# Attention in runs of two steps: a changed order of scores, row maxima and values on one core

## What is computed

```python
x = group_norm(input, gn_weight, gn_bias)            # B = 2, C = 128, 32 x 32
qkv = einsum('bchw,oc->bohw', x, qkv_weight)
q, k, v = split(qkv.reshape(B, 4, 96, 32, 32), 3, axis=2)
attn = einsum('bnchw,bncyx->bnhwyx', q, k) / sqrt(C)
attn = softmax(attn over all 1024 places y, x)
out = einsum('bnhwyx,bncyx->bnchw', attn, v).reshape(B, C, 32, 32)
out = einsum('bchw,oc->bohw', out, out_weight) + out_bias
x = out + input
# then: t = tokens(x); t = t + linear_attention(layer_norm(t)); t = t + experts(layer_norm(t))
```

## Time and profile before

| | |
|---|---|
| median of 3 runs | 360.91 us (359.94 to 361.03) |
| the profiled execution | 360.62 us, span 358.9 us |
| PE busy | 315.1 us (88%) |
| DVE busy | 202.1 us (56%) |
| ScalarE busy | 194.5 us (54%) |
| GpSimd busy | 113.7 us (32%) |
| steps 0 to 31, with row maxima | some 45 to 132 us of the span |
| steps 32 to 63, with layer 1 of image 0 | 132 to 203 us |

### The profile page before, as it was taken

One profiled execution on the slowest core, in us unless ns is written; L12 is line 12 of the kernel. 1 busy time (PEld: TensorE's weight loads), 2 busy tenths in 40 slices (PEclk: granted clock), 3 DMA queues, 4 the chain that ended last, 5 costly groups with the idle time before them and its releaser, 6 DMA issues.

```text
span 358.9 us, 6251 instructions
## 1 busy us (share of the span) xinstructions
PE 315.1 (88%) x1885; PEld 197.5 (55%) x1885; DVE 202.1 (56%) x620; ACT 194.5 (54%) x303; POOL 113.7 (32%) x190
## 2 busy tenths in 40 slices
PE   7979898899999989999999878796545599999986
PEld 3533443343444435355443336785444499999985
DVE  2585456475766753465747746766752057776610
ACT  1470676477676754546667320647332277777722
POOL 2073094000000000100031884015277745656630
PEclk9995999899999999999999998897858599999999
DMA  6069785835000007000000112100011422224215
GB/s 197 4 132 207 161 206 234 231 87 211 2 2 3 3 18 219 0 2 1 2 0 0 55 37 61 38 0 22 10 52 52 111 61 63 76 76 132 77 55 211
DMA packets 20540, 27.88 MB, mean 78 GB/s; under 512 B 3831, under 2 KB 14508, under 8 KB 20252
## 3 DMA queue, kind: packets, MB, share of 16 engines
q1 hardware_dynamic: 15800, 17.57, 18.3%
q0 software_dynamic: 3520, 9.39, 8.3%
q10 hardware_dynamic: 1188, 0.53, 0.6%
HBM read 11.15 MB, written 8.33 MB: 54 GB/s over the span
## 4 chain that ended last, share of the span: by engine, by line
PE 63%; issue 11%; POOL 11%; DVE 8%; ACT 3%; DMA 3%; SPq 0%; DVEq 0%; ACTq 0%; POOLq 0%
PE ps L913 14%; POOL expert_in L530 9%; PE ps L1132 8%; PE ps L1112 8%; PE ps L890 8%; PE ps L871 4%; PE ps L855 4%; PE ps L750 2%; PE ps L790 2%; PE ps L822 2%; POOL rstd L466 1%; DMA Qs<-mrow 1%; DVE pm L1247 1%; PE ps L1091 1%; PE ps L1163 1%
## 5 line engine op out<-in xcount | busy, mean ns | idle before, releaser
L598 ACT ACTIVATE probs<-ps 128x1024 f32<-128x1024 f32 x64 | 65.3, 1020 | 35.1 <-PE ps L890 35.0
L913 PE MATMUL ps<-probs,vT 128*32 128x512 f32 x256 | 68.6, 612 | 0.6 <-ACT probs L598 0.5
L913 PE MATMUL ps<-probs,ones 128*32 128x512 f32 x256 | 68.6, 612 | 0.0
L466 POOL TENSOR_TENSOR rstd<-ve,minus_half 128x1 f32<-128x1 f32 (+2 forms) x6 | 10.3, 1724 | 147.4 <-DVE ve L1298 77.3
L1112 PE MATMUL ps<-w,GT 128*128 x312 | 45.9, 294 | 12.0 <-ACT GT L728 11.7
L1244 DVE CUSTOM_DVE_ANT_0 above<-ps,above 128x512 f32<-128x512 f32 x56 | 38.6, 691 | 29.9 <-PE ps L871 27.4
L1112 PEld LDWEIGHTS ps<-w,GT 128*128 128x128 f32 x312 | 41.5, 207 | 13.6 <-issue 13.5
L1132 PE MATMUL ps<-XTT,w1s 128*128 128x128 f32 x312 | 46.2, 296 | 2.9 <-issue 2.7
L536 POOL DMA_INDIRECT token_out<-Y,yidx x39 | 37.7, 966 | 33.4 <-DVE Y L1571 28.7
L890 PE MATMUL ps<-Qs,Ks 98*128 98x512 f32 x128 | 43.6, 421 | 2.3 <-DMA Qs<-mrow 1.6
L1132 PEld LDWEIGHTS ps<-XTT,w1s 128*128 128x128 f32 x312 | 42.6, 211 | 4.3 <-issue 3.9
(11 more groups left out here) (224 smaller groups left out, 440.1 us busy)
## 6 DMA issues: line engine op xcount, KB each, us to landing
XR<-expert_in SPq DMA_DIRECT2D x39, 65.0 KB, 1.9
Qs<-q_hi SPq DMA_DIRECT2D x16, 128.0 KB, 3.1
w<-in_L_ffn_W SPq DMA_DIRECT2D x1, 2048.0 KB, 8.5
w<-in_L_ffn_W SPq DMA_DIRECT2D x8, 256.0 KB, 4.5
YG<-token_out SPq DMA_DIRECT2D x8, 256.0 KB, 3.9
Ks<-k_hi SPq DMA_DIRECT2D x14, 128.0 KB, 2.7
expert_in<-zeros POOLq DMA_DIRECT2D x1, 1300.0 KB, 5.6
expert_in<-zeros POOLq DMA_DIRECT2D x1, 1235.0 KB, 8.1
```

The source lines that it names most:

```text
L598: nc.scalar.activation(probs[:, s % 3, :], bank(2 + 2 * (s % 2), 2), ACT.Exp).then_inc(exp_done, 1)
L913: last = nc.tensor.matmul(bank(value_bank(o))[i * HD:(i + 1) * HD, :], w, probs[:, s % 3, hd * HALF:(hd + 1) * HALF], start=kt == 0, stop= ...
```

## The change

The order in which PE, ScalarE and DVE walk through the steps; no operation is added or removed. `pair_slots(s)` gives the new slots of steps s and s + 1 together, four or three.

- PE goes by two steps: first product of the first slot, scores of s + 1, its second product; first product of the second slot, scores of s + 2, its second product; then both products of the third and of the fourth slot; then, with the parts of layer 1 that belong to each, the values of s and the values of s + 1.
- ScalarE takes the positive parts of the first two slots behind the exp of the even step and those of the others behind the exp of the odd step; a part of layer 1 stands ahead of them.
- The "rows" of block 1 stand one place sooner in the list of slots.
- DVE's copy of the summed values stands behind the step's slots instead of behind its first one.

```diff
@@ order of slots
         for k in range(1, 2 * UNITS):
-            order.insert(min(RING * (k + 1) + 2, len(order)), (k, "rows"))
+            order.insert(min(RING * (k + 1) + (1 if k == 1 else 2), len(order)), (k, "rows"))
...
+        def pair_slots(s):
+            return range(slots_by(s), slots_by(s + 2))
@@ ScalarE
             for s in range(UNITS * STEPS):
                 exps(s // STEPS, s % STEPS)
-                if s:
-                    for g in new_slots(s - 1)[1:]:
-                        max_above(g)
                 run_parts(layer1, LAYER1_AT, s, 0)
-                for g in new_slots(s)[0:1]:
+                for g in pair_slots(s - 1)[2:] if s % 2 else pair_slots(s)[0:2]:
                     max_above(g)
@@ PE
-            for s in range(UNITS * STEPS):
-                new = new_slots(s)
-                for g in new[0:1]:
-                    max_first(g)
-                if s + 1 < UNITS * STEPS:
+            def both_scores(s):
+                if s < UNITS * STEPS:
                     for hd in range(2):
-                        scores((s + 1) // STEPS, (s + 1) % STEPS, hd)
-                for g in new[0:1]:
-                    max_second(g)
-                for g in new[1:2]:
-                    max_first(g)
-                if s == BEGIN_LAYER1:
-                    pe.wait_ge(consts_ready, 2)
-                    pe.wait_ge(ld_rows, 16 * 4)
-                run_parts(layer1, LAYER1_AT, s, 0)
+                        scores(s // STEPS, s % STEPS, hd)
+
+            def both_values(s):
                 for hd in range(2):
                     values(s // STEPS, s % STEPS, hd)
-                for g in new[1:2]:
-                    max_second(g)
+
+            for s in range(0, UNITS * STEPS, 2):
+                new = pair_slots(s)
+                for i in range(2):
+                    for g in new[i:i + 1]:
+                        max_first(g)
+                    both_scores(s + 1 + i)
+                    for g in new[i:i + 1]:
+                        max_second(g)
                 for g in new[2:]:
                     max_first(g)
                     max_second(g)
+                run_parts(layer1, LAYER1_AT, s, 0)
+                both_values(s)
+                if s + 1 == BEGIN_LAYER1:
+                    pe.wait_ge(consts_ready, 2)
+                    pe.wait_ge(ld_rows, 16 * 4)
+                run_parts(layer1, LAYER1_AT, s + 1, 0)
+                both_values(s + 1)
@@ DVE
                     norm_sums(o)
-                if s % KT == KT - 1 and s // KT < COPIED:
-                    values_copy(s // KT)
                 for g in new[1:2]:
                     max_slot(g)
...
                 for g in new[3:]:
                     max_slot(g)
+                if s % KT == KT - 1 and s // KT < COPIED:
+                    values_copy(s // KT)
```

## The result

The changed kernel took 367.37 us (median of four, 365.09 to 369.02) against 360.97 for the kernel before on the same chip, a ratio of 1.0196 (95% interval 1.0155 to 1.0238). The forecast was 362.7 with a range of 359.5 to 366.0: slower was right, by how much was not, and the time lies outside the range. The profiled execution took 367.15 us (span 365.4).

The account below looks back on a forecast made before the run. TensorE, busy 88% of the span, was taken as the bound. First half from pair 5 +3.1, start -0.2, second half -0.8, tail 0: +2.1 on 360.62 gives 362.7 us, range 359.5 to 366.0.

Parts of the forecast that it names:

- The run of maxima: First half from pair 5 on: waits in the run outweigh the changes saved, full pairs 5.82 us, +3.1 us.
- Rival 1: First half: the run finds its banks free, full pairs take 4.9 us, some -8.2, 354.5 us; chance 0.12.
- rival 3: Row lands at 65.7 because of GpSimd's zeros (+1.8), or values behind values take 0.54 (+2.5); chance 0.18.
- Pairs 0 to 2: Start: pairs 0 and 1 lose 0.8 us; pair 2 takes 5.3 against 6.2, -0.9.
- whether it is held or not: Pair 2: two values matmul groups cover VectorE's operation on the maxima even if GpSimd's fill delays it; -0.9 us.
- The row of maxima: Pair 3: row issued sooner lands at 63.9 after 5.8 us, PE waits 1.6; 8.4 us against 8.6.
- 1.0 for the part of the low clock that isn't spent in waits: Pair 3, behind the row's landing: low clock adds 1.0 us to the time until the pair ends at 69.3.
- The second half: Steps from 32: six pairs save -1.8 us, later counts and key waits cost some back; -0.8 us.
- the end follows the counts: Tail: the end depends on the counts, not the loop's end; seven steps behind them stay hidden, 0 us.
- the pair of 5.8: Full pair in the first half: last second product waits for a positive part behind an exp; pair lasts 5.8 us.
- two V at 1.89: End of each pair: two steps' values matmuls in succession take 1.89 us, at 0.45 per round.
- the wait of the key transposes: Step 43: key transposes wait for a VectorE add, losing the scores that stood between; +0.45 us.

Follow-up runs that it names:

- first half alone: Changed kernel with steps 32 to 63 back in the order of the kernel before: 364.27 us, ratio 1.0121.
- ScalarE's other order: Changed kernel with the third slot's positive part ahead of the odd step's exp on ScalarE: 364.95 us, ratio 1.0113; with GpSimd's fills after block 1's row, 358.92 us.
- twos up to 55: Kernel before with steps 32 to 55 walked in pairs and GpSimd's zero fills issued behind block 1's row of maxima: 355.37 us, ratio 0.9868.
- extra products: Changed kernel with six identity products on PE ahead of the scores of step 8, while PE waits for the row: 365.96 us, ratio 1.0143.
- the second half alone: Kernel before with only steps 32 to 63 in pairs: 360.98 us, ratio 1.0026; with GpSimd's fills behind block 1's row as well, 358.16 us, 0.9952.
- late fills: GpSimd's zero fills wait for block 1's row instead of block 0's: kernel before 357.66 us (0.9935), changed kernel 361.22 us (1.0052).
- the changed kernel's second measurement: The changed kernel run once more, unchanged, against the kernel before: ratio 1.0188.

## Why the prediction was wrong

**The run of maxima: right.** Pairs 5 to 15 took 60.16 us (79.14 to 139.30) against 57.4, +2.8 where +3.1 was forecast; 60.0 with the first half alone. Named were the wait, its place behind the exp and its length (5.82 against 5.80), and the run with ScalarE's other order takes that wait away and gains what it left. Rival 1, that nothing takes the place of the changes removed, is out. So is the dearer V behind V of rival 3 (0.54). The rounds of a V behind a V lie 0.43 apart, a little under the 0.45 that the prediction took as the least.

**Pairs 0 to 2: right, with a disturbance.** Without low clock there (first half alone) pairs 0 and 1 lost 0.7 (0.8 forecast). Pair 2 gained 1.2 (0.9 forecast), and by the cause that was named: two V cover the split of the maxima, "whether it is held or not". In the new order the pair takes 4.99 us with the split held (2.07, first half alone) and without (0.17, the profiled run). In the old order it takes 6.2 with the split held (2.11 in the kernel before, 2.12 with twos up to 55) and 4.95 without (0.17, in two other profiles), so the gain is there only where the split falls into GpSimd's memset of the zeros. The profiled run had low clock from 47 to 54 us and lost 3.6 in pairs 0 and 1. The stretch belongs to neither order: it is in three of eight profiles with the new first half and in three of five with the old one. A further 1.05 us were lost ahead of 41 us, before anything that was changed.

**The row of maxima: the step that failed.** "With the same 5.8 us it lands at 63.9" counted the landing from the row's own issue. It goes by GpSimd's fills. In eight profiles with the fills in their place the row was issued anywhere from 57.7 to 61.6, and it landed 8.9 to 9.2 us behind the fills' issue; with the fills behind it it took at most 3.0. Where the start was undisturbed (first half alone) the issue came even sooner than forecast, at 57.73 where the copy was to end at 58.1, and the row landed at 65.5 all the same. So moving the slot sooner gained nothing, while PE came to the scores one V poorer. That is the first part of rival 3, which named the fills and priced them at +1.8; both parts of that rival together had a chance of 0.18.

The second half of the same step was mis-sized too: "1.0 for the part of the low clock that isn't spent in waits". The low clock lasted into step 9 and caught two V at 3.57 instead of 1.85; with the clock kept up by extra products, the stretch is 2.5 to 3 us shorter. Before, two windows were low and one V stood in them. With the first half alone the scores come 1.6 us later than 63.9, and from them to the end of pair 4 go 12.1 us where 10.4 were set (2.45, 1.89, 1.0 and 5.1): the late landing and the low clock have about equal parts in the miss.

Together: by the ratios, the row is worth 1.0188 - 1.0052 = 1.4% in the changed kernel and 0.65% in the kernel before; the difference, 0.7% or 2.6 us, is what the row cost the new order more than the old one, where 8.4 against 8.6 us, -0.2, had been set for pair 3. The intervals leave 2.4 us or more on either side of it, so by times alone it is barely clear of nothing. The profiles carry it: pairs 3 and 4 lost 3.5 us with the first half alone and 3.0 with the "rows" at the old place. The changed kernel's own profile has only 1.15 there, since its start was late and PE came late to the row. That its wait of 1.27 looks like the forecast's 1.6 is luck.

**The second half: right up to the counts, wrong behind them.** -0.80 was forecast and -0.80 measured in six profiles with twos to the end. The other three, the changed kernel's two and that with the "rows" at the old place, have +0.5, with the low clock at 190 to 194; why it falls there is open. And "the end follows the counts" failed: with twos to the end the tail is 1 to 4 us longer (167.1 to 169.95 in nine profiles, against 166.0 to 166.3 in three with the old order there; only the profile of the kernel before has 168.7 with it). By times, the second half alone is 0.17% above the kernel before with the fills late in both, not 0.2% below, though these intervals overlap. That the steps behind the counts do it is shown by the run with twos up to 55, which keeps a gain (0.67% less than the kernel before with late fills; the intervals are apart). By which path they do it is only argued: the loop ends sooner, the inverse root keeps its place in GpSimd's order, PE idles 3.8 instead of 2.5 us, and low clock follows more often.

**The sum.** With ratios against the same before: the order in the first half costs 1.0052 - 0.9952 = 1.0%, 3.6 us (3.0 forecast for the run and pairs 0 to 2, 3.9 without the gain of pair 2); the second half costs 0.9952 - 0.9935, +0.6 instead of -0.8, which the intervals don't tell apart; the row +2.6 instead of -0.2. These shares add up to the 6.8 us of the changed kernel's second measurement (1.0188) because they are cut from it; the first (1.0196) gave 7.1. The range was too narrow on one side because it added the row's landing and its low clock as small, separate costs; both come from one wait, and both went the same way.

Of the signs named ahead, the pair of 5.8, two V at 1.89, a low clock behind the row and the wait of the key transposes came. The wait for the row was 1.27 in the changed kernel and 3.1 to 3.8 in three kernels whose start had no low clock, not some 1.6; the counts came 7.8 later instead of 2.

## What to carry to other kernels

Price a small transfer that others wait for by what was issued ahead of it on any queue, not by its own issue; if its landing stays put when it is issued sooner, move the large transfer behind it (here 0.65% in the kernel before). A wait of PE can cost its length and a low clock behind it; here the same row cost 3.0 us in one order and 6.3 in the other, so weigh a wait by what is queued behind it. Don't read a stretch of low clock in one profile as the order's doing before it has come in other kernels with the same code there. Grouping operations of one shape saves the changes between shapes but gathers operations that share banks into one run; count bank by bank and reader by reader whether the run still finds its banks free, and group only where it does.

## What the runs showed of the hardware

A row of maxima, two DMAs of 4 KB each on SP's queue, landed at most 3.0 us behind its issue when nothing large was in flight ahead, and 4.8 to 7.9 us behind it when GpSimd's two fills (1300 and 1235 KB) had been issued 1.1 to 4.4 us sooner on another queue; the landing stayed at 8.9 to 9.2 us behind the fills. It is the data that wait: the row's first packet moved 3.0 to 4.9 us behind the issue instead of 1.3, and its last one 0.4 to 0.8 us behind the last piece of the fills. The Trainium skill, DMA: Bandwidth & Descriptors, Queues, rings and completion order, says that each DMA engine takes turns between the queues that have work, packet by packet. How many of a fill's pieces make up one packet, and so whether one such turn is as long as this wait, the traces do not tell.

The granted clock fell to 0.50 behind the row in all six profiles in which PE waited 1.3 to 3.8 us for it, and stayed there for 3.4 to 6.8 us (by the trace's clock records) while PE was full again. With extra products in the same wait it stayed at 1.00. The Trainium skill, TensorE: Matmul & The Clock Gate, Part 1, says that the gate follows how busy the array has been; this pair of runs agrees.

VectorE's operation on the maxima (128x8) takes 0.17 us by itself, and 2.0 to 2.4 us in seven profiles in which it met the beginning of GpSimd's memset of the zeros (2.27 us); it ended where the memset ended.
